# Two DFTs along the image width as row tiles of 64 contracted rows

## The reference, cut to what matters

```python
xf = jnp.fft.rfft2(x, norm='forward')
top = jnp.einsum('bixy,ioxy->boxy', xf[:, :, :hm0, :hm1], w1)
bot = jnp.einsum('bixy,ioxy->boxy', xf[:, :, -hm0:, :hm1], w2)
out_fft = out_fft.at[:, :, :hm0, :hm1].set(top)
out_fft = out_fft.at[:, :, -hm0:, :hm1].set(bot)
return jnp.fft.irfft2(out_fft, s=(h, w), norm='forward')
...
x = x + _L0_conv_ref(_ln_c(x), L0_conv_w1_real, ...)
```

## Time and profile before

| | |
|---|---|
| median of 3 runs | 614.54 us (613.46 to 614.82) |
| profiled execution | 614.5 us, which is its span; nothing lies around it |
| TensorE busy | 565.0 us, 92% |
| VectorE, ScalarE, GpSimd busy | 351.7, 319.6, 115.1 us |
| forward DFT loop, about | 15 to 42.6 us of the span |
| inverse DFT loop, about | 153 to 173 us of the span |
| convolution sweeps (line 745), by the chain | 38% of the span |

### The profile page before, as it was taken

The page is one execution under the profiler, slowest core; times in us unless marked ns, Lnnn a source line. Parts: engine busy times, 40 slices in busy tenths (PEclk is TensorE's granted clock), DMA queues, the critical chain, the costliest instruction groups (busy, mean ns, idle before and its releaser), DMA issues.

```text
span 614.5 us, 22679 instructions
## 1 busy us (share of the span) xinstructions
PE 565.0 (92%) x9860; PEld 511.2 (83%) x9860; DVE 351.7 (57%) x813; ACT 319.6 (52%) x842; POOL 115.1 (19%) x240
## 2 busy tenths in 40 slices
PE   8978878999999899997999999969999999984997
PEld 8978877999998897797899988868888888984973
DVE  2657989557435943755455455435555455568736
ACT  4766979452348610254444444424445777568610
POOL 4000000000016000000233333383332034371000
PEclk9999999899999798998899999989999999998989
DMA  9830764060000000000000003340000144500007
GB/s 352 330 137 2 276 234 181 2 246 29 1 2 1 2 3 19 0 1 0 3 5 3 5 3 89 90 105 4 4 3 5 25 76 83 102 1 1 2 3 273
DMA packets 50250, 41.53 MB, mean 68 GB/s; under 512 B 44998, under 2 KB 45126, under 8 KB 48934
## 3 DMA queue, kind: packets, MB, share of 16 engines
q1 hardware_dynamic: 49304, 38.51, 19.4%
q0 software_dynamic: 704, 1.18, 0.9%
q10 hardware_dynamic: 144, 0.39, 0.2%
HBM read 27.49 MB, written 4.19 MB: 52 GB/s over the span
## 4 chain that ended last, share of the span: by engine, by line
PE 76%; DVE 12%; ACT 5%; POOL 4%; issue 2%; DMA 1%; SPq 0%; POOLq 0%; ACTq 0%
PE PS L745 38%; PE PS L458 6%; PE PS L714 5%; DVE RB L986 4%; PE PS L479 3%; PE PS L533 3%; PE PS L664 3%; PE PS L608 2%; PE PS L557 2%; PE PS L564 2%; POOL RCD L400 2%; POOL RE L397 2%; PE PS L578 2%; PE PS L638 2%; DVE sums L1025 1%
## 5 line engine op out<-in xcount | busy, mean ns | idle before, releaser
L745 PE MATMUL PS<-RE,conv_sb 128*64 128x64 f32 x6048 | 230.9, 229 | 5.1 <-DVE RE L1129 4.7
L745 PEld LDWEIGHTS PS<-RE,conv_sb 128*64 128x64 f32 x6048 | 205.3, 139 | 30.8 <-DVE RE L1129 5.4
L879 ACT COPY PS<-convb_sb 128x64 f32<-128x64 f32 x504 | 108.2, 215 | 113.3 <-DVE RE L1141 89.2
L1141 DVE SCALAR_TENSOR_TENSOR RE<-PS,RCD 128x64 f32<-128x64 f32 x252 | 56.6, 225 | 58.2 <-PE PS L745 50.1
L409 POOL COPY RCD<-RE 128x128 f32<-128x128 f32 x126 | 37.0, 294 | 166.6 <-DVE RE L1141 166.4
L1141 DVE SCALAR_TENSOR_TENSOR RE<-PS,RE 128x64 f32<-128x64 f32 x126 | 32.5, 258 | 27.9 <-PE PS L745 19.9
L808 ACT COPY RB<-PS 32x256 f32<-32x256 f32 x64 | 42.4, 662 | 7.5 <-PE PS L517 6.8
L986 DVE COPY RB<-PS 32x256 f32<-32x256 f32 x64 | 42.2, 659 | 6.0 <-PE PS L517 5.2
L1141 DVE SCALAR_TENSOR_TENSOR RE<-PS,RB 128x64 f32<-128x64 f32 x126 | 28.3, 225 | 28.1 <-PE PS L745 19.9
L479 PE MATMUL PS<-warm 128*128 128x128 bf16 x468 | 37.8, 253 | 7.1 <-ACT RCD L848 4.5
L533 PE MATMUL PS<-RE,RB 128*64 128x64 f32 x1024 | 33.6, 228 | 9.8 <-issue 4.1
(11 more groups left out here) (120 smaller groups left out, 780.1 us busy)
## 6 DMA issues: line engine op xcount, KB each, us to landing
RE<-wspec SPq DMA_DIRECT2D x8, 2048.0 KB, 8.8
RA<-x_in SPq DMA_DIRECT2D x8, 512.0 KB, 7.5
RCD<-x_in SPq DMA_DIRECT2D x1, 4096.0 KB, 13.3
out<-RA SPq DMA_DIRECT2D x8, 512.0 KB, 2.7
RCD<-RB SPq DMA_DIRECT2D x58, 64.0 KB, 2.5
RE<-RCD SPq DMA_DIRECT2D x32, 80.0 KB, 2.6
conv_sb<-conv_w SPq DMA_DIRECT2D x1, 768.0 KB, 20.0
w_sb<-w SPq DMA_DIRECT2D x2, 264.0 KB
```

The source lines that it names most:

```text
L745: m = pe.matmul(conv_bank(s, u, c)[o:o + OC], conv_sb[:, s, d, o:o + OC], prev, start=False, stop=(d == 2), skip_group_check=True)
L879: act.copy(banks_of, convb_sb[:, s:s + 1].unsqueeze(2).to_broadcast([P, c1 - c0, n])).then_inc(s_seed, 1)
L1141: dve.scalar_tensor_tensor(out=state[:, state_slot(s, u), b0:b1, 1:1 + HO], in0=conv_bank(s, u, c), scalar=0.0, in1=row_at(SRC[s], s, q, u ...
```

## The change

Both DFTs are issued as two matmuls for each block, one for partitions 0 to 63 and one for partitions 64 to 127, each with one 64 x 64 quarter of the table. The quarters of zeros are no longer used. The two results go to two banks: the first image row of all eight blocks into one bank, the second into the other, 64 columns for each block. So the order inside a pair of banks changes, and the two readers follow it: `f1_pairs` becomes two copies (real and imaginary parts, `r`) whose innermost index `a` steps from bank to bank in PSUM, with the height innermost in `RC` as it lies there; the sum on VectorE reads PSUM and writes `RC` in runs of 64.

```diff
         def f1_pairs(g, i):
-            o = RC.rearrange("p (t k r h) -> p t h r k", t=BH, k=KY, r=2)[:, g // 4, 16 * (g % 4):16 * (g % 4) + 16]
-            return [(o, i.rearrange("p (h r k) -> p h r k", r=2, k=KY))]
+            o = RC.rearrange("p (t k r h) -> p t k r h", t=BH, k=KY, r=2)[:, g // 4, :, :, 16 * (g % 4):16 * (g % 4) + 16]
+            return [(o[:, :, r].rearrange("p k (n a) -> p k n a", a=2),
+                     i.rearrange("p (a n r k) -> p r k n a", a=2, n=8, r=2)[:, r]) for r in range(2)]
...
             def dft_w(g):
                 for n in range(8):
-                    m = pe.matmul(blk(ln_slot(g), n), blk(RD, 8 * g + n), fwd_w, start=True, stop=True)
+                    for a in range(2):
+                        row = slice(W * a, W * (a + 1))
+                        m = pe.matmul(PS[:, 2 * (g % 4) + a, W * n:W * (n + 1)], blk(RD, 8 * g + n)[row],
+                                      fwd_w[row, row], start=True, stop=True)
                 return m
...
                 for n in range(8):
-                    m = pe.matmul(blk(dft_slot(g), n), blk(RB, 8 * g + n), inv_w, start=True, stop=True)
+                    for a in range(2):
+                        row = slice(W * a, W * (a + 1))
+                        m = pe.matmul(PS[:, 4 + 2 * (g % 2) + a, W * n:W * (n + 1)], blk(RB, 8 * g + n)[row],
+                                      inv_w[row, row], start=True, stop=True)
                 m.then_inc(s_if1, 1)
...
-                x1 = RC[:, 1024 * g:1024 * g + 1024]
-                dve.tensor_tensor(x1, dft_slot(g), x1, ALU.add).then_inc(s_res, 1)
+                x1 = RC[:, 1024 * g:1024 * g + 1024].rearrange("p (n a w) -> p n a w", a=2, w=W)
+                dve.tensor_tensor(x1, dft_slot(g).rearrange("p (a n w) -> p n a w", a=2, w=W), x1,
+                                  ALU.add).then_inc(s_res, 1)
```

## The result

The changed kernel takes 625.47 us in the median (621.97 to 629.85, 4 runs); the kernel before takes 614.26 us beside it. The ratio is 1.0192, with a 95% interval from 1.0150 to 1.0235. Forecast were 616.6 us, a ratio of 1.0034: the sign is right and the time lies in the range, but the loss is five times the one worked out, and above the forecast's own range (613.8 to 619.8).

The account below looks back on a forecast made before the run. TensorE was taken to pace the inverse loop fully and the forward loop about half, with ScalarE's last drain counting in full. Inverse +1.8 and forward +0.3 gave +2.1 us on 614.5: 616.6 us, range 605.5 to 628.

Parts of the forecast that it names:

- the forecast's own range: Whole kernel: 613.8 us with free shape changes and a cheap drain, 619.8 with dear ones.
- The pace of a group: Each DFT group, both loops: 32 row-tiled passes, loads in pairs of 112 ns, still take 1.79 us.
- The argument from rows: DFT groups: profile rows show loads priced by columns, not rows, and two tiles loading side by side; 1.79 us a group.
- The rivals on the group (0.94 us, 3.58, 5.4): DFT group: half-length 0.94 us, chance 0.10; loads in turns 3.58, 0.20 including partial overlap; no overlap 5.4, 0.02.
- The change of shape: Between row-tiled and full-array groups: 0.30 us a round trip; inverse loop +1.8 us, forward loop +0.7.
- The drain: ScalarE's last copy pair of the forward DFT: 1.54 us instead of 1.92, so -0.4 us.
- the bound of 1.19: Forward DFT drain, lower bound: two contiguous copies of 512 elements at 597 ns each, 1.19 us.
- Inverse loop +1.8, forward loop +0.7 - 0.4 = +0.3: Both DFT loops: shape changes +1.8 us inverse and +0.7 forward, cheaper forward drain -0.4; +2.1 us in all.
- anything else (clock, fetch): Whole kernel: leftover case for causes outside the forecast and named rivals, no size given; chance 0.03.
- a partial overlap of two loads: DFT groups: between paired loads and loads in turns, one microsecond per about 4 ns of pair pitch, below 628; chance 0.06.
- The 0.2% that the prediction took for the noise: Whole kernel: about 1.2 us is what a measurement can tell from no change; "same" means 613.3 to 615.8 us.

## Why the prediction was right in sign and wrong in size

**The pace of a group: right.** The argument from rows gave 1.79 us; 3.74 for two groups is 1.87, less the change of shape into them about 1.8. Doubling the streamed columns and halving them left it where it was. The load row of the inverse loop after, for the earlier trace rows:

```profile
L614 PEld LDWEIGHTS PS<-dft_sb,RB 64*128 64x128 f32 x256 | 14.8, 188 | 1.5 <-issue 1.0 <-ACT RB L834 0.5
```

The mean is 188 ns where it was 192, with half the rows, and 256 loads keep the load path busy for the 14.8 us of 128 before: they lie in pairs. The rivals on the group (0.94 us, 3.58, 5.4) are refuted by its 1.93 us. The page "TensorEngine Tiling (Array Packing)" of the Trainium skill, section "Theoretical Speedup", gives up to 2x where one dimension is at most 64, as the contracted one is here; the trace shows no gain for row tiles, and 1.79 to 1.09 us for tiles that halve the loaded columns as well.

**The change of shape: right.** 0.30 us a round trip, measured 2.95 - 2.66 = 0.29; six of them in the inverse loop, 1.8 forecast and 1.73 measured (1.58 in the six periods of groups by turns, and 0.15 in the last two DFT groups, which the sum had at nothing). In the forward loop +0.7 was forecast; with the same drain, 24.61 and 24.65 us with row tiles at clock 1.00 stand against 24.03 without, +0.6.

**The drain: right in kind, mis-sized.** 1.54 us taken, 1.07 measured, below the bound of 1.19; two copies of 587 ns take 1.07 us together, so the second starts before the first has ended on the timeline. The page "Advanced Engine Details and Errata" of the Trainium skill, section "PSUM Cachelines", wants every two consecutive elements contiguous for best throughput, and names matmuls as what slows down. For ScalarE and VectorE reading PSUM the runs show no such price (587 ns for 512 elements taken from two banks by turns, 1224 for 1024 at a step on VectorE).

**The step that failed** is "Inverse loop +1.8, forward loop +0.7 - 0.4 = +0.3": the forward term takes TensorE's 2.4 GHz for granted. It measured +5.37 in the profile; with the clock at 1.00, in the run with doubled streaming, it measured -0.2 (24.61 us against 24.82), and the 5.6 between are the clock. What could have been seen: the text itself noted that streaming is halved while the group's time stays, and that TensorE waits before several forward groups; it watched the clock only in the loop without waits, the inverse one, and gave "anything else (clock, fetch)" 0.03.

That 625.47 lies between 605.5 and 628 is luck. The range reached to 628 for a partial overlap of two loads, which did not come; the lower clock had no term in the sum, and three of the changed kernel's eight runs (628.41, 629.85 and 631.72 us) lie above the range.

**From the profiles to the medians.** The two spans are 5.7 us apart: +5.4 and +1.7 in the loops, and -1.4 in the rest, which the change does not touch. The medians are 11.2 apart. In every run recorded with both, the time is 1.8 to 1.9 us more than the span; so something does lie around the span, and the profiled execution of the kernel before took about 616.3 us (an estimate from its 614.5), 2.0 above its median. The changed kernel's profiled one, 621.97, is 3.5 below its median. The other runs of the changed kernel have lower mean clocks, 0.953 to 0.937; where theirs fell is not shown. The 0.2% that the prediction took for the noise was too little as well: 25 runs of the kernel before on one chip went from 610.1 to 619.6 us.

**Not settled.** Both loops in row tiles with streaming doubled end about 2 us over their loops' sum, within the interval, and this was not followed up. The inverse loop alone ends 1.5 us over its 1.73; the stretch at clock 0.57 costs 1.65 in the profiled execution, and whether the other runs have it is not known. And what, besides halved streaming, brings the lower clock in one execution and not in the next is open.

## What to carry to other kernels

Before splitting an fp32 matmul into tiles, find what paces its passes. Where the load is as long as the pass, as here, tiles of half the rows brought nothing but changes of shape, and only tiles with fewer loaded columns made the group shorter (1.09 us). Work that TensorE is relieved of beside a wait may be paid back at the lower clock, in groups that were not touched: look at the granted clock of each loop, not at its mean over the kernel. And where a copy out of PSUM must reorder, put the step on the PSUM side and write runs.

## What the runs showed of the hardware that was not expected

Streaming 64 columns of zeros more for each pass shortened a loop by 5.6 us (30.19 to 24.61), and streaming 64 fewer on the full array, in groups of the same length, brought stretches near the 1.2 GHz level (0.55 from 17 to 24 us). The kernel before's own loop, in another run, was followed by one too (0.57 from 42 to 46 us), behind a wait of 1.96 us that left the clock at 1.00 in the profile before. Four tiles of 64 by 64 do an fp32 pass in 17 ns, 64 passes in 1.09 us. A copy of 512 elements that takes one from each of two PSUM banks by turns takes 587 ns on ScalarE; the copy with the step on the SBUF side took 1919 ns for 1024.
